# Copies of the sort's turned blocks moved from VectorE to ACT, in fixed chunks of the convolution's tiles

## The chip, the cores and the metric

The kernel runs on one core of one Trainium2 chip. The metric is the device time of one execution in microseconds (us). A core has five engines that run their own instruction streams and meet by semaphores: PE (TensorE, matrix products), VectorE (DVE), ACT (ScalarE), POOL (GpSimd) and SP (SyncE, here an issuer of transfers). Each works through its own stream in order: an instruction that waits holds up what stands behind it on its engine.

## The reference

The whole network is a convolution layer of 32 paths, an attention layer with a 7 x 7 window, and a graph layer with experts:

```python
x = _L0_conv_ref(x, ...)                  # 32 paths: 1x1 to 4 channels, 3x3, 1x1 to 64, each with norm and relu; sum + x, relu
t = _to_tokens(x)
t = t + _L1_attn_ref(_ln_t(t), ...)
t = t + _L1_ffn_ref(_ln_t(t), ..., L1_ffn_edge_index)   # graph attention over 262144 edges, then two of four experts a token
```

The graph layer sums over the edges that end in a node (`segment_sum(..., dst)`). The kernel sorts the 262144 edges by their end for it, and does that sort while the convolution of the first six images runs.

## The kernel before

`conv_phase` is called twice. The first call takes six images of 56 x 56 pixels, seven tiles of eight rows each, 42 tiles, and carries the sort; the second takes the last two images later and has no sort. All loops over tiles are written out, so each engine has one long fixed order of instructions.

**A tile of the convolution.** PE expands a stack of 75 rows to the 32 paths' 64 channels in 16 chunks (`expand`, L570), two chunks into each of two PSUM tiles `psE`. VectorE folds each pair of chunks with relu into `acc` (L882 for the first pair of a tile, L885 for the other seven). So a pair (called duo in the code) can be expanded only when the fold two pairs before has freed its PSUM tile. Between the chunks PE does other things of the tiles around: the nine taps of the 3 x 3 convolution of the tile three ahead, one behind each of chunks 4 to 12 (L553); the sum of the tile before (`to_tokens`, L593) behind chunk 3; the turn of its normalised tokens to channels behind chunk 4 (L604); the projection of the tile two before (L610, L615) behind chunk 13.

Each tile's layer norm goes through three engines. VectorE adds the residual (L825) behind its second fold; ACT takes relu with a sum (L689). VectorE makes the negated mean (L830) behind its fourth fold, that of chunks 6 and 7; ACT's squares of the tile (L697) wait for it. Variance (L834) and inverse deviation (L838, L840) follow behind the sixth and eighth fold.

ACT's order in a tile is fixed too: relu of the reduced input (L659), the normalised tokens (L707), a part of the split of a later tile and its store, relu with sum (L689), the copy of turned tokens (L712), squares (L697), `stack_parts` (nine transfers that load the stack of the tile two ahead, issued from ACT's queue at L682), relu behind the taps (L665, L667), the projection's copies (L719, L722, L727), the deviation (L702).

**The sort.** `Sort.plan` is a bitonic sort over 128 partitions of 2048 keys, in two buffers `sort_key` and `sort_other`. A compare step is two VectorE instructions of 1024 columns, the minima (L276) and the maxima (L278); signs and negations are single ones. Where the network compares across partitions, the whole array is turned: PE transposes blocks of 128 x 128, four at a time, into one PSUM bank `psFV` (`turn`, L316), and VectorE copies the bank out into the other buffer with a strided target (`copy_back`, L284). One turn is four such rounds, and there are 14 turns, 56 rounds. There is one bank for this, which `to_tokens` and `project` use as well: a round waits until the copy of the round before is done.

The 417 entries of the list (361 VectorE instructions, 56 rounds) are spread over slots of the tiles. The first 26 run ahead of the tiles. Slot `at` of a tile stands ahead of VectorE's fold `at // 2`; eleven slots a tile are in use, all of 2 to 13 but 4, and `schedule` gives one to a VectorE instruction and two to a round (the copy stands in the second, PE's turn behind the chunk one before it). So rounds can fall on any of chunks 1 to 12, one to three chunks apart, also ahead of the sum behind chunk 3.

Of the kernel before, what the change touches and what calls it, by code (L numbers as in the profile page):

```python
# [20 lines left out]
TILES = H // ROWS  # L21
# [115 lines left out]
SORT_SLOTS = (2, 3, 5, 6, 7, 8, 9, 10, 11, 12, 13)  # L137
# [85 lines left out]
class Sort:  # L223
# [32 lines left out]
    def vector_steps(self, dve, bank):  # L256
# [23 lines left out]
        def copy_back(now, turns, r):  # L280

            dve.wait_ge(self.turn_ready, turns * self.ROUNDS + r + 1)
            size = LOW // self.ROUNDS
            dve.tensor_copy(self.buffers[1 - now][:].rearrange("h (p l) -> h l p", l=LOW)[:, r * size:(r + 1) * size, :],  # L284
                            bank[:].rearrange("h (l p) -> h l p", p=128)).then_inc(self.turn_done, 1)

        for kind, *args in self.plan:
            if kind == "turn":
                for r in range(self.ROUNDS):
                    out.append((lambda a=(now, turns, r): copy_back(*a), (now, steps, turns, r)))  # L290
                turns += 1
                now = 1 - now
                continue
            for half in range(2 if kind == "compare" else 1):
                out.append((lambda a=(kind, args, now, steps, turns, half): one(*a), None))
            steps += 1
            if kind == "compare":
                now = 1 - now
        return out

    def schedule(self, marks):

        slot, at = 0, {}
        for k, mark in enumerate(marks):
            slot += 1 if mark is None else 2
            at[slot] = k
        return at
# [12 lines left out]
def conv_phase(nc, io, images, t1_dram, q_dram, kpad_dram, vpad_dram, sorted_dram=None, gate=None, kept_ident=None):  # L320
# [3 lines left out]
    with ExitStack() as ctx:  # L324
# [62 lines left out]
        sort_slots, turn_at = {}, {}  # L387
        if sorted_dram is not None:
            sort = Sort(sort_key, sort_other, signs, stepped, turn_ready, turn_done)
            marks = [mark for _, mark in sort.vector_steps(None, None)][SORT_FIRST:]  # L390
            sort_slots = sort.schedule(marks)
        for slot, k in sort_slots.items():
            if marks[k] is not None:
                turn_at[slot // len(SORT_SLOTS), SORT_SLOTS[slot % len(SORT_SLOTS)] - 1] = marks[k]

# [41 lines left out]
        with (nc.Block() if gate is None else nullcontext(gate.block)) as block:  # L437
# [95 lines left out]
            def _(pe):  # L533
# [29 lines left out]
                def expand(n, t, taps, others):  # L563
                    g = n * TILES + t
                    pe.wait_ge(stacked[t], 16 * 9 * (n + 1))
                    for c in range(CHUNKS):
# [8 lines left out]
                        if (g, c) in turn_at:  # L575
                            wait(pe, u_done, issued["folds"])
                            wait(pe, v_done, issued["values"])
                            sort.turn(pe, psTurn, ident, *turn_at.pop((g, c)))
                            issued["rounds"] += 1
# [61 lines left out]
                assert not turn_at  # L641
# [6 lines left out]
            def _(act):  # L648
# [79 lines left out]

                def image(n, first, last):
                    for t in range(TILES):  # L730
# [11 lines left out]
                        if not (first and t == 0):  # L742
                            squares(*ahead(n, t, -1))
                        if not (last and t + 2 >= TILES):
                            stack_parts(*ahead(n, t, 2))
                        if not (last and t + 3 >= TILES):
# [27 lines left out]
            def _(dve):  # L774
# [71 lines left out]
                if sorted_dram is not None:  # L846
# [6 lines left out]
                    steps = [step for step, _ in sort.vector_steps(dve, psTurn)]  # L853
                sort_at = {slot: steps[SORT_FIRST + k] for slot, k in sort_slots.items()}

# [11 lines left out]
                def tile(n, t, pending):  # L867
                    g = n * TILES + t
                    for duo in range(DUOS):
                        for k, at in enumerate(SORT_SLOTS):  # L870
                            if at // 2 == duo and g * len(SORT_SLOTS) + k in sort_at:
                                sort_at.pop(g * len(SORT_SLOTS) + k)()
# [31 lines left out]
                for at in sorted(sort_at):  # L904
                    sort_at[at]()
# [1463 lines left out]
```

## Time and profile before

| | us |
|---|---|
| median of 3 executions (5034.34 to 5045.57) | 5041.94 |
| the profiled execution's own time | 5049.61 |
| its span, first to last instruction | 5048.0 |
| VectorE busy in the span | 2727.8 (54%) |
| PE busy in the span | 2733.0 (54%) |
| ACT busy in the span | 1504.5 (30%) |

Busy time is the union of an engine's instructions; register work, waits and the issue of transfers don't count. The span is one execution on the one core. In rows of the trace a line begins with its start in us from the span's start, then its duration, engine, line of the kernel, operation and the tensors it writes and reads; what stands in brackets is the idle time ahead of it on its engine and who ended that. PEclk and "granted clock" are shares of TensorE's full clock of 2.4 GHz: 0.50 is 1.2 GHz.

### The profile page before, as it was taken

What the parts mean: (1) busy time and instruction counts of PE and PEld (TensorE: products, weight loads), DVE (VectorE), ACT (ScalarE), POOL (GpSimd) and SP (SyncE); (2) the same over time, 40 slices, a digit from 0 to 9 for tenths busy, and PEclk for the clock granted to TensorE, in tenths of its full rate; (3) what the DMA queues carried; (4) which work ended last, traced back from release to release, by engine and by line L of the source; (5) the groups of instructions that cost most, each with busy time, mean ns of one, the idle gap of its engine ahead of it and who ended that gap; (6) DMA issues with size and microseconds to landing.
All of it is one profiled execution on the core that took longest, in us unless ns stands there. A gap on an engine that the chain in (4) does not pass through costs nothing. (4 is left out here: it accounts for less than half of the span.)

```text
span 5048.0 us, 57429 instructions
## 1 busy us (share of the span) xinstructions
PE 2733.0 (54%) x15808; PEld 1889.2 (37%) x15808; DVE 2727.8 (54%) x4352; ACT 1504.5 (30%) x5774; POOL 2782.1 (55%) x3036
## 2 busy tenths in 40 slices
PE   5888888769999777858828853101210211021222
PEld 2454454458888655634418741000000000000122
DVE  7988889849999749954556661101110111001277
ACT  1333333348888410003416622101110111011100
POOL 1000000026667537776777777777777777777473
PEclk8877888769999755558757856555555555555565
DMA  5666666546666450126734432101110111011244
GB/s 98 99 106 99 99 104 107 83 77 103 101 104 102 85 148 11 11 52 99 117 82 82 83 80 78 45 8 45 45 45 8 46 45 43 9 42 41 83 149 145
DMA packets 620524, 380.12 MB, mean 75 GB/s; under 512 B 431448, under 2 KB 552344, under 8 KB 617656
## 3 DMA queue, kind: packets, MB, share of 16 engines
q1 hardware_dynamic: 425208, 223.43, 19.5%
q10 hardware_dynamic: 94368, 109.47, 12.4%
q0 software_dynamic: 100768, 45.27, 7.4%
q8 instruction: 58, 0.95, 0.1%
q14 instruction: 122, 1.00, 0.1%
HBM read 232.92 MB, written 144.35 MB: 75 GB/s over the span
## 5 line engine op out<-in xcount | busy, mean ns | idle before, releaser
L1603 POOL DMA_INDIRECT e_row<-scratch_table,e_edge x2048 | 2011.3, 982 | 680.9 <-issue 678.4
L1968 PE MATMUL f_psY<-f_hid,f_w 128*64 128x512 f32 x392 | 126.8, 745 | 1460.4 <-ACT f_hid L1928 1460.4
L1777 DVE TENSOR_TENSOR e_e<-e_row,e_b 128x512 f32<-128x512 f32 x16 | 11.3, 704 | 1528.1 <-DMA e_row<-scratch_table,e_edge 1527.8
L1968 PEld LDWEIGHTS f_psY<-f_hid,f_w 128*64 128x64 f32 x392 | 35.8, 157 | 1538.6 <-ACT f_hid L1928 1527.0
L1031 POOL MEMSET a_wproj<- 128x128 f32 x1 | 0.2, 209 | 1025.8 <-POOLq L179 1025.8
L1184 ACT ACTIVATE prob<-psS,low 128x100 f32<-128x100 f32 x1568 | 512.5, 371 | 104.2 <-DVE low L1219 102.6
L553 PE MATMUL psH<-h,c_w 128*128 128x448 f32 x1008 | 513.9, 602 | 8.1 <-ACT h L659 4.5
L1119 PE MATMUL psS<-keys,q_exp 84*128 84x100 f32 x3136 | 419.8, 288 | 156.9 <-DMA keys<-in_kfeat 154.0
L885 DVE SCALAR_TENSOR_TENSOR acc<-psE,acc 128x896 f32<-128x896 f32 x392 | 425.3, 1085 | 112.4 <-PE psE L570 105.2
L1119 PEld LDWEIGHTS psS<-keys,q_exp 84*128 84x128 f32 x3136 | 404.5, 208 | 161.1 <-issue 154.1
L1809 ACT ACTIVATE e_weight<-e_drop 128x1024 f32<-128x1024 f32 x16 | 16.9, 1056 | 1470.9 <-DVE e_drop L1790 1470.9
L570 PE MATMUL psE<-stack,c_w 75*128 75x448 bf16 x896 | 345.0, 429 | 158.6 <-DVE acc L885 128.8
L1184 ACT ACTIVATION_READ_ACCUMULATOR prob<-psS,low 128x1 f32 x1568 | 367.7, 234 | 0.0
L1701 DVE TENSOR_TENSOR i_hot<-i_values,i_digit 128x1024 bf16<-128x1024 bf16 x512 | 319.3, 700 | 0.3 <-DVE i_values L1693 0.3
L1219 DVE TENSOR_REDUCE low<-psS 128x5 f32<-128x500 f32 x336 | 212.5, 641 | 155.1 <-PE psS L1119 147.8
L1730 PE MATMUL i_psC<-i_hot 128*128 128x128 bf16 x2048 | 255.8, 298 | 71.7 <-DVE i_hot L1701 71.7
L553 PEld LDWEIGHTS psH<-h,c_w 128*128 128x128 f32 x1008 | 219.2, 218 | 122.0 <-issue 111.0
L1195 ACT ACTIVATE prob_t<-psP 100x512 f32<-100x512 f32 x448 | 227.6, 578 | 106.4 <-PE psP L1133 106.3
L1133 PE MATMUL psP<-a_ident,prob 128*100 128x128 f32 x1568 | 234.9, 292 | 37.2 <-ACT prob_t L1195 32.0
L1730 PEld LDWEIGHTS i_psC<-i_hot 128*128 128x128 bf16 x2048 | 190.1, 133 | 137.4 <-DVE i_hot L1701 137.4
L1028 POOL DMA_DIRECT2D scratch_t<-t x168 | 113.2, 678 | 193.3 <-DVE t L1261 99.1
L570 PEld LDWEIGHTS psE<-stack,c_w 75*128 75x128 bf16 x896 | 87.3, 112 | 348.5 <-issue 157.6
(297 smaller groups left out, 5507.7 us busy)
## 6 DMA issues: line engine op xcount, KB each, us to landing
stack<-scratch_parts ACTq DMA_DIRECT2D x504, 112.0 KB
e_row<-scratch_table,e_edge POOLq DMA_INDIRECT x2048
val<-scratch_vpad SPq DMA_DIRECT2D x784, 35.0 KB
scratch_y<-f_y ACTq DMA_DIRECT2D x49, 512.0 KB, 2.7
scratch_state<-e_state SPq DMA_DIRECT2D x16, 1536.0 KB, 6.3
g_y<-scratch_y SPq DMA_DIRECT2D x24, 1024.0 KB
scratch_parts<-h2p ACTq DMA_DIRECT2D x56, 336.0 KB, 6.4
keys<-scratch_kpad SPq DMA_DIRECT2D x112, 155.0 KB
```

What stands on the lines that cost most here:

```text
L553: m = pe.matmul(psH2[:, 0:PIX].rearrange("p (y x) -> p y x", x=W), w2[:, tap, :], h1[:, ROWS * t + dy:ROWS * (t + 1) + dy, dx:dx + W], sta ...
L570: m = pe.matmul(psE[duo % 2][:, half, 0:PIX], w3[:, c, :], stack[third(n, t)][:, c, :], start=True, stop=True)
L885: dve.scalar_tensor_tensor(acc[:, third(n, t)], e, 0.0, acc[:, third(n, t)], ALU.max, ALU.add).then_inc(stt_done, 1)
L1119: m = pe.matmul(psS[bank][:, (blk - a) * KEYS:(blk - a + 1) * KEYS], q_exp[st.pair][:, par, blk].rearrange("k h m -> k (h m)"), keys[st.at ...
L1133: m = pe.transpose(psP[k % 2][0:KEYS, (blk - a) * 128:(blk - a + 1) * 128], prob[par][:, blk * KEYS:(blk + 1) * KEYS], ident[:])
L1184: m = act.activation(prob[par][:, blk * KEYS:(blk + 1) * KEYS], psS[bank][:, (blk - a) * KEYS:(blk - a + 1) * KEYS], ACT.Exp, bias=low[par ...
L1195: act.activation(prob_t[:, a:b, :], psP[k % 2][0:KEYS, 0:(b - a) * 128].rearrange("k (b m) -> k b m", m=128), ACT.Copy).then_inc(pt_done, 1)
L1219: dve.tensor_reduce(low[par][:, a:b], psS[bank][:, 0:(b - a) * KEYS].rearrange("p (b k) -> p b k", k=KEYS), AX.X, ALU.min)\
L1603: pool.indirect_dma_start(out=self.row[s][:, f, :], out_offset=None, in_=self.table_dram, in_offset=bass.IndirectOffsetOnAxis(ap=self.edge ...
L1701: m = dve.tensor_tensor(hot[g % 2][d][:], values[:].unsqueeze(1).to_broadcast([128, HOT // 2, 128, 2]), digit[par][:, d, g * HOT:(g + 1) * ...
L1730: m = pe.matmul(psC, hot[g % 2][1][:, c // 2, :, c % 2], hot[g % 2][0][:, c // 2, :, c % 2], start=False, stop=False)
L1968: m = pe.matmul(psY[par][half:half + C, e // 2, :], w2[:, e, :], hid[e][:], start=True, stop=True)
```

## The change

The copies of the turned blocks go from VectorE to ACT (`copy_back` is now called in ACT's stream, by `copies_back`). Rounds may stand only behind chunks 6 to 11 of a tile (`ROUND_AT`), one chunk apart; VectorE steps may use all of the slots 2 to 13, also slot 4. `schedule` now walks both lists: a turn's first round comes at least two slots behind the step ahead of it, and a step at least three behind the last round. In ACT's order the copies of rounds behind chunks 6 and 7 stand between the squares and `stack_parts`, those behind chunks 8 to 11 between `stack_parts` and the relu behind the taps. By the new plan the sort's last step stands in tile 41, the last; before it stood in tile 40.

```diff
-SORT_SLOTS = (2, 3, 5, 6, 7, 8, 9, 10, 11, 12, 13)
+SORT_SLOTS = tuple(range(2, 14))
+ROUND_AT = tuple(range(6, 12))
...
-        def copy_back(now, turns, r):
-
-            dve.wait_ge(self.turn_ready, turns * self.ROUNDS + r + 1)
-            size = LOW // self.ROUNDS
-            dve.tensor_copy(self.buffers[1 - now][:].rearrange("h (p l) -> h l p", l=LOW)[:, r * size:(r + 1) * size, :],
-                            bank[:].rearrange("h (l p) -> h l p", p=128)).then_inc(self.turn_done, 1)
-
...
     def schedule(self, marks):
 
-        slot, at = 0, {}
+        tile, free, steps, rounds = 0, 0, {}, {}
         for k, mark in enumerate(marks):
-            slot += 1 if mark is None else 2
-            at[slot] = k
-        return at
+            if mark is not None and mark[3] == 0:
+                free += 2
+            allowed = SORT_SLOTS if mark is None else ROUND_AT
+            while not any(at >= free for at in allowed):
+                tile, free = tile + 1, 0
+            at = next(at for at in allowed if at >= free)
+            if mark is None:
+                steps[tile, at] = k
+            else:
+                rounds[tile, at] = mark
+            free = at + (3 if mark is not None and mark[3] == self.ROUNDS - 1 else 1)
+        return steps, rounds
+
+    def copy_back(self, act, bank, now, steps, turns, r):
+
+        act.wait_ge(self.turn_ready, turns * self.ROUNDS + r + 1)
+        size = LOW // self.ROUNDS
+        act.activation(self.buffers[1 - now][:].rearrange("h (p l) -> h l p", l=LOW)[:, r * size:(r + 1) * size, :],
+                       bank[:].rearrange("h (l p) -> h l p", p=128), ACT.Copy).then_inc(self.turn_done, 1)
...
-                        if (g, c) in turn_at:
+                        if (g, c) in rounds:
                             wait(pe, u_done, issued["folds"])
                             wait(pe, v_done, issued["values"])
-                            sort.turn(pe, psTurn, ident, *turn_at.pop((g, c)))
+                            sort.turn(pe, psTurn, ident, *rounds[g, c])
...
+                def copies_back(n, t, *at):
+                    for c in at:
+                        if (n * TILES + t, c) in rounds:
+                            sort.copy_back(act, psTurn, *rounds[n * TILES + t, c])
...
                             squares(*ahead(n, t, -1))
+                        copies_back(n, t, *ROUND_AT[0:2])
                         if not (last and t + 2 >= TILES):
                             stack_parts(*ahead(n, t, 2))
+                        copies_back(n, t, *ROUND_AT[2:])
                         if not (last and t + 3 >= TILES):
                             h2_relu(*ahead(n, t, 3))
```

On ACT, in tile 10, where the first turn stands by the new plan, the order before is this (`t` and `sq` are relu and squares of the tile before, `stack` the nine loads for the tile two ahead, `h` and `h2p` the relu behind the taps):

```order
L689 ACTIVATE t_0,stat<-usum 112x64 x4
L712 ACTIVATE z_ch<-psQK 64x448
L697 ACTIVATE sq,stat<-t_0,stat 112x64 x4
L682 DMA stack_0<-scratch_parts 8x16x448 x9
L665 ACTIVATE h_0<-psH_0,c_s_0 128x448
L667 ACTIVATE h2p<-h_0 128x448
```

And with the change (lines are numbered anew; L316 is the copy):

```order
L694 ACTIVATE t_0,stat<-usum 112x64 x4
L717 ACTIVATE z_ch<-psQK 64x448
L702 ACTIVATE sq,stat<-t_0,stat 112x64 x4
L316 ACTIVATE sort_other<-psFV 128x4x128 x2
L687 DMA stack_0<-scratch_parts 8x16x448 x9
L316 ACTIVATE sort_other<-psFV 128x4x128 x2
L670 ACTIVATE h_0<-psH_0,c_s_0 128x448
L672 ACTIVATE h2p<-h_0 128x448
```

Two copies now stand behind the squares, and two behind the nine loads. On PE, the turn that begins in tile 14 stood before as follows, from chunk 10 of tile 14 to the sum behind chunk 3 of tile 15 (`psE` are the chunks, `psH` the taps, `psFV<-c_ident` the turns):

```order
L570 MATMUL psE_0<-stack_0,c_w_0 128x448
L553 MATMUL psH_0<-h_0,c_w_0 128x448
L316 MATMUL psFV<-c_ident,sort_key 128x128 x4
L570 MATMUL psE_0<-stack_0,c_w_0 128x448
L553 MATMUL psH_0<-h_0,c_w_0 128x448
L570 MATMUL psE_0<-stack_0,c_w_0 128x448
L553 MATMUL psH_0<-h_0,c_w_0 128x448
L316 MATMUL psFV<-c_ident,sort_key 128x128 x4
...
L570 MATMUL psE_0<-stack_0,c_w_0 128x448 x3
L316 MATMUL psFV<-c_ident,sort_key 128x128 x4
L570 MATMUL psE_0<-stack_0,c_w_0 128x448
L593 MATMUL psFV<-c_fold,acc 112x64 x8
```

With the change it stands in chunks 6 to 9 of tile 14:

```order
L576 MATMUL psE_0<-stack_0,c_w_0 128x448
L559 MATMUL psH_0<-h_0,c_w_0 128x448
L326 MATMUL psFV<-c_ident,sort_key 128x128 x4
L576 MATMUL psE_0<-stack_0,c_w_0 128x448
L559 MATMUL psH_0<-h_0,c_w_0 128x448
L326 MATMUL psFV<-c_ident,sort_key 128x128 x4
L576 MATMUL psE_0<-stack_0,c_w_0 128x448
L559 MATMUL psH_0<-h_0,c_w_0 128x448
L326 MATMUL psFV<-c_ident,sort_key 128x128 x4
L576 MATMUL psE_0<-stack_0,c_w_0 128x448
L559 MATMUL psH_0<-h_0,c_w_0 128x448
L326 MATMUL psFV<-c_ident,sort_key 128x128 x4
```

The four rounds of a turn stood over two tiles, one of them ahead of the sum behind chunk 3; now they stand in neighbouring chunks of one tile, with a chunk and a tap between two of them.

## Rows read from the trace of the kernel before

**Rows 1.** Windows of stages: first:end, length, busy time (and instructions) of each engine, PEclk, transfers

```profile
core 0: us, PE busy (x) PEld busy (x) DVE busy (x) ACT busy (x) POOL busy (x), PEclk, DMA share, GB/s
...
74.62:1025.50 950.88, 795.53 (x2886) 459.70 (x2884) 855.00 (x1010) 341.87 (x1213) 0.00 (x0) 0.79 0.62 98
```

**Rows 2.** VectorE's groups in the stage: count, busy us, mean ns, idle ahead and releaser

```profile
L882 DVE TENSOR_SCALAR acc<-psE 128x896 f32<-128x896 f32 x42 | 45.5, 1083 | 9.8 <-PE psE L570 9.8
L284 DVE COPY sort_other<-psFV 128x512 f32<-128x512 f32 x28 | 28.4, 1014 | 15.5 <-PE psFV L316 15.2
L284 DVE COPY sort_key<-psFV 128x512 f32<-128x512 f32 x28 | 28.4, 1014 | 8.0 <-PE psFV L316 7.1
```

**Rows 3.** Windows of tile 13 and tile 33, columns as in group 1

```profile
371.20:393.83 22.63, 18.43 (x67) 10.18 (x66) 22.46 (x28) 8.54 (x32) 0.00 (x0) 0.80 0.69 105
...
834.65:854.28 19.63, 19.63 (x87) 12.85 (x85) 17.82 (x23) 8.40 (x32) 0.00 (x0) 0.85 0.62 97
```

**Rows 4.** Timeline of tile 33 (834.65 to 854.28) and of its successor's first product

```profile
834.69 3.11 PE L593 MATMUL psFV<-c_fold,acc 128*112 128x64 f32 x16
...
835.65 1.21 DVE L276 TENSOR_TENSOR sort_other<-sort_key 128x1024 f32<-128x1024 f32 x1
836.79 1.22 DVE L278 TENSOR_TENSOR sort_other<-sort_key 128x1024 f32<-128x1024 f32 x1
...
841.79 0.35 PE L570 MATMUL psE<-stack,c_w 75*128 75x448 bf16 x1
...
842.74 0.35 PE L570 MATMUL psE<-stack,c_w 75*128 75x448 bf16 x1
...
843.68 0.61 PE L316 MATMUL psFV<-c_ident,sort_other 128*128 128x128 f32 x4
...
844.13 0.35 PE L570 MATMUL psE<-stack,c_w 75*128 75x448 bf16 x1
...
844.14 0.16 DVE L830 TENSOR_SCALAR stat<-stat 112x4 f32<-112x4 f32 x1
...
844.33 0.35 ACT L697 ACTIVATE sq<-t,stat 112x64 f32<-112x64 f32 x1 [2.87 <-DVE stat L830]
...
845.00 0.27 ACTq L682 DMA_DIRECT2D stack<-scratch_parts  x1
...
845.58 0.19 ACT L697 ACTIVATION_READ_ACCUMULATOR sq<-t,stat 112x1 f32 x1
...
845.68 2.67 ACTq L682 DMA_DIRECT2D stack<-scratch_parts  x7
...
848.80 0.35 PE L570 MATMUL psE<-stack,c_w 75*128 75x448 bf16 x1
...
851.27 2.28 DVE L885 SCALAR_TENSOR_TENSOR acc<-psE,acc 128x896 f32<-128x896 f32 x2
...
851.73 0.55 PE L570 MATMUL psE<-stack,c_w 75*128 75x448 bf16 x2
...
853.99 1.70 PE L593 MATMUL psFV<-c_fold,acc 128*112 128x64 f32 x16
```

**Rows 5.** Timeline of a turn that waited for a VectorE step

```profile
501.40 1.28 DVE L271 TENSOR_SCALAR sort_other<-sort_other,signs 128x2048 f32<-128x2048 f32 x1
...
502.94 0.69 PE L316 MATMUL psFV<-c_ident,sort_other 128*128 128x128 f32 x4 [2.00 <-DVE sort_other L271]
...
503.67 1.01 DVE L284 COPY sort_key<-psFV 128x512 f32<-128x512 f32 x1
```

**Rows 6.** ACT's groups by form: a copy of 512 columns out of PSUM

```profile
L1547 ACT ACTIVATE t_z_ch<-t_psZ 64x512 f32<-64x512 f32 x28 | 16.4, 586 | 4.3 <-PE t_psZ L1519 4.3
```

**Rows 7.** Waits in the stage: who waited for whom, total us, times, longest us

```profile
ACT sq L697 <- DVE stat L830: 161.6, 41, 4.9
```

**Rows 8.** Windows of tile 33 before and after its change of clock, columns as in group 1

```profile
834.65:840.59 5.94, 5.94 (x26) 4.78 (x25) 5.22 (x7) 2.10 (x10) 0.00 (x0) 0.50 0.98 150
840.59:854.28 13.69, 13.69 (x63) 8.07 (x61) 12.59 (x16) 6.30 (x23) 0.00 (x0) 1.00 0.46 75
```

More of the change, by code:

```diff
@@ L254, in __init__, with vector_steps @@
         self.steps = sum(step[0] != "turn" for step in self.plan)
-    def vector_steps(self, dve, bank):
+    def vector_steps(self, dve):
         now, steps, turns = 0, 0, 0
@@ L289, in vector_steps @@
                 for r in range(self.ROUNDS):
-                    out.append((lambda a=(now, turns, r): copy_back(*a), (now, steps, turns, r)))
+                    out.append((None, (now, steps, turns, r)))
                 turns += 1
@@ L386, in conv_phase @@
         turn_ready = sem("turn_ready"); turn_done = sem("turn_done")
-        sort_slots, turn_at = {}, {}
+        sort_slots, rounds = {}, {}
         if sorted_dram is not None:
             sort = Sort(sort_key, sort_other, signs, stepped, turn_ready, turn_done)
[L390 to L394, printed above, removed]
+            sort_slots, rounds = sort.schedule([mark for _, mark in sort.vector_steps(None)][SORT_FIRST:])
         psH1 = ps("psH1", [128, 512])
@@ L640, in _ @@
                     image(n, n == 0, n == N - 1)
-                assert not turn_at
                 to_tokens(N - 1, TILES - 1)
@@ L852, in _ @@
                     dve.wait_ge(built, 2)
-                    steps = [step for step, _ in sort.vector_steps(dve, psTurn)]
+                    steps = [step for step, _ in sort.vector_steps(dve)]
                 sort_at = {slot: steps[SORT_FIRST + k] for slot, k in sort_slots.items()}
+                assert all(g < N * TILES for g, at in sort_at)
                 def rest(n, t):
@@ L869, in tile @@
                     for duo in range(DUOS):
-                        for k, at in enumerate(SORT_SLOTS):
-                            if at // 2 == duo and g * len(SORT_SLOTS) + k in sort_at:
-                                sort_at.pop(g * len(SORT_SLOTS) + k)()
+                        for at in SORT_SLOTS:
+                            if at // 2 == duo and (g, at) in sort_at:
+                                sort_at.pop((g, at))()
                         if g + 2 < N * TILES:
@@ L903, in _ @@
                     op()
-                for at in sorted(sort_at):
-                    sort_at[at]()
+                assert not sort_at
         if gate is None:
```

## Prediction

> **What bounds the kernel now.** I read the windows by stage first. The stretch from the first to the last fold of the early convolution takes 950.88 us, and VectorE is busy in 855.00 of them (90%), more than any other engine [rows 1]; what comes behind the stage in the span of 5048.0 us holds none of the changed code. So only this stage can move, and VectorE is its bound, with 95.9 us of idle time in it. Then I read VectorE's groups: the 56 copies that the change takes away are 2 x 28.4 us of busy time, and VectorE stood 15.5 + 8.0 us in front of them [rows 2]. Last I read single tiles. A tile with eleven sort steps and no round is VectorE's alone: 22.46 busy of 22.63 us. A tile with four rounds is not: in tile 33 (834.65 to 854.28) PE is busy for all of its 19.63 us and VectorE for 17.82 [rows 3]. So the copies cost VectorE's time in some tiles, and in tiles with rounds the order of PE and of what PE waits for decides. That is where the change has to be priced.
>
> **What the new plan makes of the tiles.** By the new schedule the same 335 VectorE steps and 56 rounds fall into three kinds of tile. 25 tiles have no round (17 of them twelve steps). Nine (10, 11, 14, 18, 22, 32, 34, 37, 39) have two steps, at slots 12 and 13, and four rounds, at chunks 6 to 9. Eight have something between: 15 and 19 four rounds and four steps, 23 and 24 two rounds, 27 and 29 three, 26 and 28 one. What VectorE saves: a copy lasts 1.014 us [rows 2], and neighbours overlap by some 0.08 us (a step lasts 1.21 us, the next starts 1.14 later [rows 4]), so 56 x 0.934 = 52.3 us of busy time go. The other term is the idle time in tiles with rounds, worked out by walking through one.
>
> **A tile of two steps and four rounds.** I use tile 33, whose PE work is the same (four rounds, at chunks 5, 7, 9 and 11, and three steps, at slots 2, 3 and 13), and count from its start at 834.65. PE reaches the second turn at 843.68, that is at 9.03 [rows 4], with one turn and the products of chunks 4 to 7 before it, exactly what stands before it in the new order. In the new order this turn needs the first copy, and on ACT that copy stands behind the squares of the tile before. The squares wait for VectorE's negated mean, which comes behind the fold of chunks 6 and 7: it starts at 844.14, the squares at 844.33, and the last of them ends at 845.77, at 11.12 [rows 4]. This is no accident of one tile: ACT waited for that value 41 times, 3.9 us each on average [rows 7]. So the first copy starts at 11.12, some 3 us after its block is turned (PE does that before chunk 7, which starts at 842.74, at 8.09).
>
> What a copy costs on ACT no row shows. Low end: ACT copies 512 contiguous columns out of PSUM in 0.586 us [rows 6]. High end: VectorE's copy with the very same strided target, 1.014 us [rows 2]. VectorE passes 896 contiguous columns of PSUM in 1.083 us [rows 2], so 512 would be 0.62, and the stride costs it 0.39 us; I add these to ACT's 0.586 and take 0.98 us, nearer to the row with the same target. The Trainium skill prices it too (ScalarE: Activation LUTs, What ACT_TABLE_LOAD costs): 186 ns and 0.833 ns a column with immediate scale and bias, an estimate of 0.61 us here, with no word of the target's stride. The contiguous row agrees with it; by it alone the sum below would be about 10 us lower.
>
> The copy ends at 12.10. From VectorE's last write to a waiting turn the trace shows 0.26 us (502.68 to 502.94), a turn of 0.69, and 0.04 to the copy [rows 5]. The second turn thus starts at 12.36 instead of 9.03: **3.33 us late**. It ends at 13.05, ACT takes its copy at 13.09, and only then may ACT's queue issue the nine loads of the next stack that stand behind it. These nine take from 845.00 to 848.35, 3.35 us [rows 4], so the third copy, behind them, starts at 16.44 and ends at 17.42, and the fourth turn starts at 17.68. PE alone would have come to it two chunks after the second turn, at 2 x 1.39 us (842.74 to 844.13 is a chunk with tap and turn [rows 4]), at 15.14: **2.54 us late** once more. Together 5.87 us.
>
> Tile 33 starts chunk 12 at 848.80, at 14.15, with four turns behind it; here that is 20.02, and chunk 11 one pair (0.95 us, 841.79 to 842.74) earlier, with its product done at about 19.42 [rows 4]. VectorE folds chunks 10 and 11 to 20.55, makes its two steps (2 x 1.14) to 22.85, and folds the last two pairs; from the first of these to the next tile's start tile 33 needs 3.01 us (851.27 to 854.28). The tile is 25.86 us long. PE doesn't prolong it: its chunks 14 and 15 end 3.48 us after chunk 12 starts (848.80 to 852.28), at 23.5, and VectorE wants them at 23.95. VectorE's own work in it is 22.46 - 9 x 1.14 = 12.2 us, so **13.7 us idle, nine times: 123 us**. The eight mixed tiles walked the same way, each wait where its own slots put it: 15 is 25.4 us long (bound by PE's end), 19, 24, 27 and 29 about 25, 23 is 23.2, 26 and 28 19.6; against their work 10.9, 10.5, 10.5, 11.6, 11.6, 6.5, 1.5 and 1.5 us idle, 65 us.
>
> **Sum.** 855.0 - 52.3 + 123 + 65 + 25 x 0.2 (tile 13's rest of 0.17 [rows 3]) = 995.7 us for a stage that took 950.9: **45 us longer**. The waits in front of the old copies and the folds that stood behind them are gone in this sum; they are among the 95.9 us that I replaced. The added wait on the loads of the stack costs nothing by itself: they are issued some 2 to 3 us later for a tile two tiles ahead. Twelve steps instead of eleven in a tile cost nothing beyond their own 1.14 us. The profiled execution took 5049.6 us; the median of three is 5041.9, and I put the 45 us on that: **5087 us**.
>
> Bounds. With a copy of 0.59 us the first and the third wait are 0.39 shorter in 14 tiles: -11 us. The start of tile 33 ran at 1.2 GHz for 5.94 us, with PE busy throughout [rows 8]; the same fold took 3.11 us there and 1.70 at 2.4 GHz [rows 4]. If every such tile began at 2.4 GHz its second turn could come 3.0 us earlier at most: -42 us in 14 tiles. Both together leave about -8. The other way, a fall of the clock is the second rival.
>
> **Rivals.**
> *The copies are in time* (the other side). If PE hardly waited, a tile with four rounds would be tile 33 and one step more, 20.8 us: 8.6 us idle nine times (77), about 37 in the mixed tiles: 855.0 - 52.3 + 77 + 37 + 5 = 922, 29 us shorter, 5013 us. For it speaks that ACT is busy for only 8.4 us of such a tile [rows 3]. Against it, that ACT's order is fixed: the first copy can't pass the squares, nor the third the nine loads. It decides where the two waits come to 2.3 us a tile instead of 5.87. Chance 0.12.
> *The clock falls in the wait.* In tile 33 PE ran without a pause and the clock held 2.4 GHz from 840.59 to the end [rows 8]. Here PE stands for over 3 us in the middle. If the clock then went to 1.2 GHz, the 8.15 us of products from 844.13 to 852.28 [rows 4] would double, and some 3 us of that fit into the second wait and VectorE's lead: 5 us a tile, 70 us in 14, about 35 if half of them fall: 5122 us. The Trainium skill (TensorE: Matmul & The Clock Gate, Part 1) says that the throttled state is the default and activity releases it; the rows at the tile's start bear that out, none that I read shows such a pause in mid-tile. Chance 0.15.
> *The waits are there but shorter* (cheap copy, tiles that begin at 2.4 GHz, a chunk 7 that comes earlier): 3 to 25 us slower, 5045 to 5067 us. Chance 0.25, of which a third is within 0.2%.
>
> **How the numbers follow.** 0.2% (10 us) is about what a measurement of this kernel can tell from no change. My forecast, 25 to 68 us slower, has 0.48, with 5067 to 5110 as its own range. With the rivals: slower 0.78, same 0.10, faster 0.12. The range runs from 5040, which leaves out the faster rival, to 5130, which leaves out the worse half of the clock rival.
>
> **What would show it.** Right, if VectorE's busy time in the stage falls to about 803 us while the stage gets longer; if the tiles named above last about 26 us and the others about 24; if PE waits about 3 us for ACT's copy before the second turn and 2 to 3 before the fourth; and if ACT's third copy starts right behind the ninth load. Wrong, if ACT's squares end before PE has turned the first block (the negated mean comes earlier than at 9.5), if the third copy starts while the loads are still being issued, or if the tiles with rounds are under 22 us. A copy of 0.6 or 1.0 us settles the price of the stride.

## The result, and the profile after

The changed kernel takes 5094.0 us (median of four executions, 5086.52 to 5100.35) against 5043.75 us (four, 5034.34 to 5046.36): ratio 1.0096, interval 1.0083 to 1.0109. It is some 50 us slower; 5087 was predicted.

The windows of the changed kernel, columns as in [rows 1]: the stage (this window is 0.6 us wider than from the first to the last fold), a tile of twelve sort steps and no round, and a stretch of the last part of the network, long behind the stage.

```profile
73.77:1062.30 988.53, 775.37 (x2890) 433.67 (x2887) 800.61 (x955) 397.08 (x1270) 0.00 (x0) 0.82 0.60 94
...
358.90:382.55 23.65, 18.91 (x67) 10.61 (x66) 23.51 (x28) 8.54 (x32) 0.00 (x0) 0.79 0.63 103
4789.53:4826.10 36.57, 36.57 (x72) 11.90 (x72) 8.12 (x18) 17.47 (x27) 0.00 (x0) 0.64 0.29 111
```

From the first to the last fold it is 987.9 us, 37.0 us longer than the stage in [rows 1]. VectorE lost some 54 us of work (855.00 to 800.61) as the diff promises; its idle time grew from 95.9 to 187.6 us. The view of VectorE's waits says for whom it stood (who waited for whom, total us, times, longest us):

```profile
DVE acc L898 <- PE psE L576: 171.6, 60, 8.2
DVE acc L895 <- PE psE L576: 8.0, 1, 8.0
DVE h2p L878 <- ACT h2p L676: 7.0, 13, 0.9
```

Nearly all of it is the fold waiting for PE's chunks, up to 8.2 us at a time. The same view for all engines says why PE was late, and why ACT was:

```profile
ACT sq L702 <- DVE stat L842: 172.1, 41, 5.6
...
PE psFV L326 <- ACT sort_key L316: 36.9, 18, 5.2
PE psFV L326 <- ACT sort_other L316: 32.3, 13, 3.1
...
ACT sort_other L316 <- issue: 18.4, 6, 4.9
ACT sort_key L316 <- issue: 17.2, 5, 5.8
```

PE's turns stood 69.2 us for ACT's copies; ACT's squares stood 172.1 us for VectorE's negated mean (161.6 before [rows 7]); and 35.6 us ahead of a copy ACT waited for "issue", which is its own queue at the nine loads. So the ring is closed: VectorE waits for PE, PE for ACT, ACT for VectorE.

Tile 10 (309.25 to 336.02) shows it from row to row:

```profile
317.96 0.61 PE L326 MATMUL psFV<-c_ident,sort_key 128*128 128x128 f32 x4
...
319.80 0.16 DVE L842 TENSOR_SCALAR stat<-stat 112x4 f32<-112x4 f32 x1
320.00 0.35 ACT L702 ACTIVATE sq<-t,stat 112x64 f32<-112x64 f32 x1 [4.41 <-DVE stat L842]
...
321.34 1.00 ACT L316 ACTIVATE sort_other<-psFV 128x512 f32<-128x512 f32 x1
...
322.48 0.69 PE L326 MATMUL psFV<-c_ident,sort_key 128*128 128x128 f32 x4 [2.97 <-ACT sort_other L316]
...
323.21 1.03 ACT L316 ACTIVATE sort_other<-psFV 128x512 f32<-128x512 f32 x1 [0.87 <-PE psFV L326]
323.21 3.36 ACTq L687 DMA_DIRECT2D stack<-scratch_parts  x9
...
325.30 1.09 DVE L898 SCALAR_TENSOR_TENSOR acc<-psE,acc 128x896 f32<-128x896 f32 x1 [5.33 <-PE psE L576]
326.62 1.02 ACT L316 ACTIVATE sort_other<-psFV 128x512 f32<-128x512 f32 x1 [2.39 <-issue]
...
327.79 0.69 PE L326 MATMUL psFV<-c_ident,sort_key 128*128 128x128 f32 x4 [1.78 <-ACT sort_other L316]
```

The first block is turned by 318.57 and lies in the bank for 2.8 us until ACT, held in the squares, takes it out at 321.34; PE stands 2.97 us. The third copy starts at 326.62, right behind the ninth load. Something that the prediction did not have appears in tile 18 (497.8 to 525.3), where the loads themselves are late:

```profile
500.10 0.35 ACTq L680 DMA_DIRECT2D scratch_parts<-h2p  x1
...
507.57 1.02 ACT L316 ACTIVATE sort_key<-psFV 128x512 f32<-128x512 f32 x1 [0.87 <-PE psFV L326]
...
510.93 3.40 ACTq L687 DMA_DIRECT2D stack<-scratch_parts  x9
514.37 1.02 ACT L316 ACTIVATE sort_key<-psFV 128x512 f32<-128x512 f32 x1 [5.77 <-issue]
...
515.54 0.66 PE L326 MATMUL psFV<-c_ident,sort_other 128*128 128x128 f32 x2 [5.17 <-ACT sort_key L316]
```

The nine loads read what the store at 500.10 writes, and in the code ACT waits for its landing ahead of them. The view of the DMA issues gives that store 10.8 us to landing in this window:

```profile
scratch_parts<-h2p ACTq DMA_DIRECT2D x1, 336.0 KB, 10.8
```

That is 510.90, and the loads start at 510.93. ACT's queue stood from 508.59 until then with nothing to do, and the third copy behind it. So it is in four of the nine tiles with two steps and four rounds: in tiles 14, 18, 32 and 37 the loads start 0.02 us after the landing, in the other five together with the second copy.

### The profile page after: what moved, and what is told of

It is laid out like the page before. It is cut to its first block and busy times, and to the rows that moved or that the text cites. A ratio compares the mean times of both kernels' runs of the same rounds, so it can differ in the third digit from the quotient of the medians.

```text
span 5098.6 us, 57429 instructions
## 1 busy us (share of the span) xinstructions
PE 2718.7 (53%) x15808; PEld 1864.4 (37%) x15808; DVE 2674.2 (52%) x4296; ACT 1562.3 (31%) x5830; POOL 2783.9 (55%) x3036
```

## The experiments

The times of each set stand beside runs of the kernel before on the same chip (medians 5043.75 for the changed kernel, 5049.99, 5051.12 and 5050.19 us for the three sets of experiments, each of which ran on another chip), so the ratios are what is compared from set to set: 0.001 is 5 us. Stage is first to last fold, of one profiled execution each; the run on the copy's price below has the changed kernel's stage unchanged and took 984.4 us for it against 987.9, so differences of a few us of stage are not told from chance. The nine tiles are those with two steps and four rounds in the new plan.

| kernel | us | ratio, interval | stage | VectorE busy | mean of the nine |
|---|---|---|---|---|---|
| before | | 1 | 950.9 | 855.0 | 22.1 |
| changed | 5094.0 | 1.0096 (1.0083 to 1.0109) | 987.9 | 800.4 | 25.9 |
| two copies ahead of the squares | 5086.25 | 1.0069 (1.0057 to 1.0081) | 975.8 | 800.4 | 25.3 |
| two copies ahead of the loads | 5068.94 | 1.0034 (1.0018 to 1.0051) | 964.0 | 800.2 | 22.6 |
| both | 5036.09 | 0.9973 (0.9963 to 0.9983) | 935.0 | 801.2 | 20.5 |
| new plan, copies on VectorE | 5022.56 | 0.9942 (0.9928 to 0.9956) | 924.2 | 850.3 | 20.4 |
| all four ahead of the squares | 5047.27 | 0.9994 (0.9983 to 1.0004) | 941.0 | 802.4 | 20.6 |
| two chunks apart | 5067.97 | 1.0039 (1.0025 to 1.0054) | 955.8 | 801.3 | (another plan) |
| two apart, all ahead of the loads | 5081.26 | 1.0064 (1.0051 to 1.0077) | 981.4 | 800.7 | (another plan) |
| changed, neighbours together | 5082.35 | 1.0066 (1.0053 to 1.0079) | 976.5 | 799.7 | 25.3 |
| both, neighbours together | 5032.34 | 0.9963 (0.9950 to 0.9975) | 935.2 | 801.2 | 20.3 |
| copies on VectorE, neighbours together | 5020.37 | 0.9945 (0.9934 to 0.9957) | 918.0 | 833.9 | 19.9 |

**The theory** is that of the prediction: ACT's fixed order makes PE wait twice in a tile of rounds. Rivals: the new plan's crowding of four rounds into one tile costs the time whoever copies; the copy's price on ACT does; the clock does.

### The first wait alone: two copies ahead of the squares

```diff
+                        copies_back(n, t, *ROUND_AT[0:2])
                         if not (first and t == 0):
                             squares(*ahead(n, t, -1))
-                        copies_back(n, t, *ROUND_AT[0:2])
```

> Changed kernel, but in ACT's order the copies of the rounds behind chunks 6 and 7 stand ahead of the squares; those of chunks 8 to 11 stay behind the nine loads. Theory A (the two places in ACT's order cost the time): the second turn starts about 9.4 us into a tile with four rounds instead of 12.4, but the squares and with them the nine loads end only 1.2 us earlier, and the fourth turn waits for them: 1.2 us less in nine tiles and some in the mixed ones, 12 to 20 us less than the changed kernel, about 33 us above the kernel before (5077). The stage (first to last fold) about 972 us. Theory B (the pace: rounds one chunk apart, each behind a copy of 1.02 us, whatever stands around them): within 8 us of the changed kernel, about 47 above before. Theory C (PE's clock falls while it waits): the time follows the granted clock in the tiles with rounds.

The stage is 12.1 us shorter than the changed kernel's, the ratio 0.0027 (14 us) lower. The first copies now come at once, but the time saved is partly given back at the second wait. Tile 14 of this kernel starts at 401.1:

```profile
408.16 1.02 ACT L316 ACTIVATE sort_other<-psFV 128x512 f32<-128x512 f32 x1 [0.87 <-PE psFV L326]
...
409.33 0.68 PE L326 MATMUL psFV<-c_ident,sort_key 128*128 128x128 f32 x4 [0.26 <-ACT sort_other L316]
...
413.91 3.34 ACTq L687 DMA_DIRECT2D stack<-scratch_parts  x9
417.30 1.02 ACT L316 ACTIVATE sort_other<-psFV 128x512 f32<-128x512 f32 x1 [6.91 <-issue]
418.46 1.09 PE L326 MATMUL psFV<-c_ident,sort_key 128*128 128x128 f32 x4 [7.51 <-ACT sort_other L316]
```

PE is done with its third turn at 410.01, 8.9 us into the tile, and behind one more chunk and tap it stands 7.51 us ahead of the fourth: the store of this tile, issued at 403.4, landed 10.5 us later, and nothing behind the loads could start before. The loads start at the landing in eight of the nine tiles now, and most of the first wait has moved to the second: in the nine tiles PE's waits ahead of the second turn fall from 27.5 to 3.1 us in all, and those ahead of the fourth grow from 21.4 to 44.1. All of PE's waits for copies in this stage, 69.2 us before the edit, come to 59.7:

```profile
PE psFV L326 <- ACT sort_key L316: 34.2, 19, 7.0
...
PE psFV L326 <- ACT sort_other L316: 25.5, 18, 7.5
```

### The second wait alone: two copies ahead of the loads

```diff
                         copies_back(n, t, *ROUND_AT[0:2])
+                        copies_back(n, t, *ROUND_AT[2:])
                         if not (last and t + 2 >= TILES):
                             stack_parts(*ahead(n, t, 2))
-                        copies_back(n, t, *ROUND_AT[2:])
```

> Changed kernel, but all copies of a tile stand between the squares and the nine loads. Theory A: the first wait stays (second turn at 12.4 or later), the third copy follows its turn at once and the fourth turn starts at about 16.3 instead of 17.7: 12 to 18 us less than the changed kernel, about 35 us above the kernel before. The nine loads are issued 3 us later, with no effect. Theory B: within 8 us of the changed kernel. A rival on the loads: if their issue were the tight part, the tile two later would wait for its stack and the time would rise above the changed kernel.

23.9 us off the stage, 0.0062 (31 us) off the ratio, more than the 12 to 18 us that were expected. PE's waits for copies fall by about as much as the stage, to 44.9 us:

```profile
PE psFV L326 <- ACT sort_key L316: 22.5, 13, 3.7
PE psFV L326 <- ACT sort_other L316: 22.4, 13, 3.0
```

What is left is the first wait, which is the larger of the two in all; removed alone, it gave only 12.1 us of stage because the second took most of it back.

### Both

The first two copies ahead of the squares, the other two between squares and loads.

> Changed kernel, with the copies of chunks 6 and 7 ahead of the squares and those of chunks 8 to 11 between the squares and the nine loads. Theory A: both waits shrink, the fourth turn starts at about 13.9 instead of 17.7; 42 to 50 us less than the changed kernel, which is more than the sum of the two single edits (24 to 38), because in each of them the other wait takes over; within 15 us of the kernel before. Theory B: 10 to 15 us less than the changed kernel at most. Theory C: the gain goes with a higher granted clock in the tiles with rounds.

52.9 us off the stage, 0.0123 (62 us) off the ratio. That is more than the two edits apart (12.1 + 23.9), as the first one's gain needs the second: what an edit is worth hangs on the order, 12.1 and then 40.8 us of stage, or 23.9 and then 29.0. The new plan with the copies on ACT is faster than the kernel before now (0.9973). PE's waits for copies, which were 69.2 us:

```profile
PE psFV L326 <- ACT sort_key L316: 9.8, 21, 1.2
PE psFV L326 <- ACT sort_other L316: 5.8, 18, 0.5
```

They fell by 53.6 us, the stage by 52.9. Since chunk for chunk the rounds stand as in the changed kernel, the plan's crowding is not what cost the time there. The stage's granted clock is 0.83 against 0.82, but single tiles differ: in the changed kernel the clock falls to 1.2 GHz in the middle of seven of the nine (11, 14, 18, 22, 32, 34 and 37); here those seven hold 2.4 GHz from 7 us on until 17.7 us or later. So the falls of the clock come and go with the waits and are a part of their price; the part on why the prediction was right says how large.

### The plan alone: copies back on VectorE

```diff
-        act.activation(self.buffers[1 - now][:].rearrange("h (p l) -> h l p", l=LOW)[:, r * size:(r + 1) * size, :],
-                       bank[:].rearrange("h (l p) -> h l p", p=128), ACT.Copy).then_inc(self.turn_done, 1)
+        dve.tensor_copy(self.buffers[1 - now][:].rearrange("h (p l) -> h l p", l=LOW)[:, r * size:(r + 1) * size, :],
+                        bank[:].rearrange("h (l p) -> h l p", p=128)).then_inc(self.turn_done, 1)
...
+                            if at // 2 == duo and (g, at - 1) in rounds:
+                                sort.copy_back(dve, psTurn, *rounds[g, at - 1])
```

ACT's two calls of `copies_back` are left out.

> The changed kernel's plan (rounds behind chunks 6 to 11, steps in all slots from 2 to 13), but the copies made by VectorE again, each in the slot behind its round; ACT as in the kernel before. Theory A: no copy stands behind squares or loads, so a tile with four rounds lasts about 21.4 us; VectorE has its 52 us of copies back; all in all 0 to 15 us below the kernel before, so some 55 us less than the changed kernel. Theory B: the copy costs 1.01 us on VectorE as 1.02 on ACT and the rounds are as close together, so about the time of the changed kernel, 40 to 50 us above before.

More than that: 27 us under the kernel before, and by the medians under every version with the copies on ACT (the interval of the nearest, 0.9963 in the table, overlaps with this one's by 0.0006). The window of its stage (0.6 us wider than first to last fold), and VectorE's wait for the chunks in it:

```profile
73.96:998.79 924.83, 758.00 (x2889) 422.88 (x2887) 850.54 (x1011) 339.23 (x1214) 0.00 (x0) 0.84 0.65 100
```

```profile
DVE acc L898 <- PE psE L576: 16.3, 15, 2.7
```

VectorE does 49 us more work here than with both earlier places on ACT, and the stage is 10.8 us shorter. So the change falls into two parts: the new plan gives 26.7 us of stage (950.9 to 924.2), and handing the copies to ACT where the diff puts them takes 63.7 (924.2 to 987.9). In the nine tiles of four rounds, 20.4 us long on average, PE is busy for 18.5 us and VectorE, copies and all, for 16.2, so its copies can cost little there. Why the plan itself gains was not taken apart: it packs the rounds, uses slot 4 and has no round ahead of the sum behind chunk 3 any more, where PE waited 15.9 us for copies in the kernel before (8.8 and 7.1 us, by its view of waits) and waits for none here.

### All four ahead of the squares

> The changed kernel with all copies of a tile ahead of the squares, and so ahead of the nine loads. Theory A: nothing is left in front of a copy but its own turn, so it is the lower end for copies on ACT in this plan; against the kernel with both edits only the third copy could gain (its turn waited 0.1 to 0.2 us for the squares there), while the squares now end some 3 us later and VectorE's variance behind the sixth fold may wait up to 1 us: within 8 us of that kernel, 5 to 20 us below the kernel before. If it came out clearly faster than the kernel with both edits, the squares still held copies up there; if slower, the variance waits.

It is 6.0 us of stage and 0.0021 (11 us) of the ratio worse than with two of them behind. PE's wait for copies hardly differs (12.7 against 15.6 us); but now the squares wait for the last round, and VectorE's variance for the squares:

```profile
DVE stat L846 <- ACT sq L702: 9.1, 5, 2.9
```

With two behind the squares that wait was at most 1.5 us, so it could cover the 6 us; but PE's wait for input tiles that SP's queue loads (`x_tok`) is 4 us longer here too (13.6 against 9.6), and no run tells the two apart.

### The price of the copy

At the end of the stage of the changed kernel, 24 more copies from the bank, four of each form: 512 elements side by side; every second; every fourth, eighth, sixteenth (rows of 128, as in the kernel's own copy); and every sixteenth group of four neighbours, written neighbour after neighbour:

```diff
+    act.activation(flat[:, 0:128 * stride].rearrange("h (p l) -> h l p", l=stride)[:, 0:4, :],
+                   psTurn[:].rearrange("h (l p) -> h l p", p=128), ACT.Copy)
+    act.activation(flat[:, 0:2048].rearrange("h (p l) -> h p l", l=16)[:, :, 0:4],
+                   psTurn[:].rearrange("h (l p) -> h p l", p=128), ACT.Copy)
```

> The changed kernel with 24 more copies at the very end of ACT's stream in the stage, out of the sort's PSUM bank into a buffer no longer needed, each waiting for the one before; four of each kind, 512 columns: contiguous target; stride of 2; four runs of 128 with a stride of 4, 8 and 16 (the last is the sort's own pattern); and the sort's own target written four neighbours at a time, the source strided instead. They change nothing that is computed. If the stride is what makes ACT's copy 1.02 us, the contiguous one takes 0.59 to 0.65 us and the price rises with the stride up to 1.02 at 16; if it is the bank, the partitions or ACT itself, all kinds take about 1.02. In the last kind neighbours are written together: 0.6 to 0.7 us if the order of writes counts, 1.0 if the span does. The time is that of the changed kernel and some 20 us.

Groups of ACT by line (duration ns min/median/max): side by side; every second; the three larger strides together; neighbours together.

```profile
L788 ACT ACTIVATE h<-psFV x4: 591/597/597, 1075.6 to 1077.5; 128x512 f32<-128x512 f32 x4
```

```profile
L790 ACT ACTIVATE h<-psFV x4: 619/619/619, 1078.1 to 1080.1; 128x512 f32<-128x512 f32 x4
```

```profile
L793 ACT ACTIVATE h<-psFV x12: 1023/1066/1084, 1080.7 to 1092.8; 128x512 f32<-128x512 f32 x12
```

```profile
L796 ACT ACTIVATE h<-psFV x4: 597/597/597, 1093.8 to 1095.7; 128x512 f32<-128x512 f32 x4
```

Its single run took 5097.25 us. The price is not one of distance: between strides of 8 and 16 bytes it jumps from 0.62 to 1.07 us, and stays within 1.02 to 1.08 at 16, 32 and 64 bytes. Writing four neighbours one after the other brings it back to 0.60, though PSUM is then read 128 columns apart; nor are the shorter runs the reason, as this form has the shortest. The Trainium skill (SBUF — State Buffer, Door 1: The DMA port swizzle, the remark on lines) says that accesses which follow one another run at full rate when at least two fall in the same line of 16 bytes. The rows agree on both sides of that step.

The same order of writing in the kernels:

```diff
-        act.activation(self.buffers[1 - now][:].rearrange("h (p l) -> h l p", l=LOW)[:, r * size:(r + 1) * size, :],
-                       bank[:].rearrange("h (l p) -> h l p", p=128), ACT.Copy).then_inc(self.turn_done, 1)
+        act.activation(self.buffers[1 - now][:].rearrange("h (p l) -> h p l", l=LOW)[:, :, r * size:(r + 1) * size],
+                       bank[:].rearrange("h (l p) -> h p l", p=128), ACT.Copy).then_inc(self.turn_done, 1)
```

In the changed kernel:

> The changed kernel with one edit: ACT's copy walks its target so that the four elements that lie side by side are written one after the other (and reads PSUM 128 columns apart), instead of 512 writes 64 bytes apart. A look at such copies alone gave 0.60 us in place of 1.02. If the copy's price is a term of the two waits in a tile with four rounds, the second and the fourth turn each come some 0.4 us earlier in 9 tiles and parts of that in the mixed ones: stage 7 to 12 us shorter than that of the changed kernel, time 5082 to 5088 us, and PE's waits for ACT's copy fall from 69 to about 57 us. Rival: only the order on ACT decides (squares, loads and the landing of the store ahead of them), and the loads take up what the copy gives back: stage within 4 us.

```profile
L316 ACT ACTIVATE sort_other<-psFV x28: 572/597/597, 321.3 to 836.4; 128x512 f32<-128x512 f32 x28
```

The stage is 11.4 us shorter, as the prediction's bound for a cheap copy had it (11 us), the ratio 0.003 lower. PE's waits fell less than expected, from 69.2 to 63.6 us and not to 57: ACT's own wait at the loads ahead of its copies grew from 35.6 to 58.3 us. So half of the 11.4 us does not show in PE's waits, and where it comes from is open. With both earlier places:

> The copies on ACT at both earlier places in its order (two ahead of the squares, two ahead of the loads), with the four neighbours written together. There PE's waits for copies are only some 16 us in all, so the copy's price can give back little: 0 to 8 us below the same kernel with the old order of writing (ratio 0.996 to 0.9975). If it gives 10 us or more, the copy's 0.4 us counts elsewhere on ACT: in the squares, the relu of the next tile and the loads behind it.

The stage is the same (935.2 against 935.0) and the times' intervals overlap: the copy's price gives nothing that this measurement can tell. PE's waits for copies did fall, from 15.6 to 3.5 us, but its waits for `x_tok` were 7.5 us longer in this profile (17.1 against 9.6), so a gain of some us may be hidden. And on VectorE:

> The new plan with the copies on VectorE, and their target walked four neighbours at a time. If VectorE's copy too is slowed by its writes 64 bytes apart, it falls from 1.01 to about 0.62 us, VectorE's busy time in the stage from 850 to about 828, and the time by 3 to 15 us below the kernel with the copies on VectorE in the old order (in tiles with four rounds PE is the bound, so most of it turns into idle time of VectorE). Rival: on VectorE the reading of PSUM 128 columns apart costs as much as the writing did, the copy stays near 1.0 and the time within 4 us.

```profile
L316 DVE COPY sort_other<-psFV x28: 681/688/693, 315.4 to 789.2; 128x512 f32<-128x512 f32 x28
```

VectorE's copy falls from 1.01 to 0.69 us, its busy time by 16 us and the stage by 6.2; the ratio (0.9945) can't be told from that without it (0.9942), and 6.2 us of stage is not far above what chance gives.

### The rounds two chunks apart

An attempt to give each copy more time, on the kernel with both earlier places: one of the later two copies ahead of the loads, one behind.

```diff
-SORT_SLOTS = tuple(range(2, 14))
-ROUND_AT = tuple(range(6, 12))
+SORT_SLOTS = tuple(range(2, 16))
+ROUND_AT = (5, 7, 9, 11)
```

> Copies on ACT, but rounds only behind chunks 5, 7, 9 and 11, two chunks apart, and VectorE steps in the slots 2 to 15 so that the sort still ends in time (tile 40); copies of chunks 5 and 7 ahead of the squares, of 9 between squares and loads, of 11 behind the loads. With a turn, a copy and the way back 1.9 to 2.0 us after another, no turn should wait for a copy. Theory A (places in ACT's order): little more to gain than from both edits, since the turns there wait only 0.5 us each; the stage 920 to 935 us, 10 to 25 us below the kernel before. Theory B in its weak form (the pace of neighbouring chunks costs a good part): well below that, under 910 us and 40 us below the kernel before.

A miss: 20.8 us of stage more than with neighbouring chunks, all of it idle time of VectorE (154.5 against 133.8 us). The first thing to suspect was the last copy behind the loads, so it was put ahead of them too:

> The rounds two chunks apart (chunks 5, 7, 9, 11) as in the run that missed, with one edit: the last copy stands ahead of the nine loads too. If that run missed because its fourth copy stood behind the loads, which wait for the landing of the store and hold the sort's last steps and PE's next use of the bank, the tiles with four rounds fall from 23.2 us on average to 20 to 21, and the time to 5035 to 5052 us. Rival: the distance of two chunks itself costs (steps pushed to the end of the tile and into other tiles, the clock): then it stays within 6 us of 5068.

That is worse by 25.6 us of stage and 0.0025 of the ratio (13 us), so the suspicion falls. Two tiles are over 30 us long there, and the view of waits names the cause of some 16 of the 25.6 us, PE's wait for the input tiles `x_tok` (24.3 us, against 8.7 in the run ahead of it):

```profile
PE psH L549 <- DMA x_tok<-in_x: 24.3, 2, 13.0
```

Why these loads landed late, and why two chunks between rounds cost 20 us in the first place, stays open. What can be seen is that most turns now spread over two tiles, that tiles without rounds get fourteen steps (25.7 us), and that the stage's granted clock is lower than with neighbouring chunks (0.79 against 0.83); no run tells these apart.

## Why the prediction was right

**VectorE's work.** 802.7 us was worked out (855.0 - 52.3), 800.4 measured.

**The copy.** 0.98 us was taken for ACT, nearer to the row with the same target than to the contiguous one; it took 1.02 (28 each at 1023 and 1022 ns). The price list above shows the reason for that choice to be sound: the order of writing sets it, on both engines (0.43 us a copy on ACT, 0.33 on VectorE, by the runs with neighbours together). The price by contiguous columns would have been out by 0.4 us a copy.

**The first wait.** Its cause is shown by the rows of tile 10 and by the edit that removes it. The second turn was put at 12.36 us into the tile; in tile 10 it starts at 13.23 (322.48). Tile 18 ran at 2.4 GHz from its start, and its second turn starts at 9.05 (506.85), 3.3 us earlier than in the sum; the prediction's bound for this was 3.0. Tiles 11, 14, 32 and 37 began like it. The wait itself was put at 3.33 us; PE stood 3.05 on average in the nine tiles (2.97 in eight of them, 3.72 in tile 39).

**The second wait came out on average, but with a cause that the prediction lacks.** The step reads: "the third copy, behind them, starts at 16.44". With 3.35 us of issue and nothing that holds the loads up, that is near in tile 10 (17.37, behind a second turn that was 0.87 late). But the loads also wait for the landing of the store that ACT's queue issued ahead of the squares, 6.5 us in the middle of 40 and up to 12.9. Before the change only the relu behind the taps stood behind this wait. In tiles 14, 18, 32 and 37, which began fast, the second copy was done 1.1 to 2.3 us before the landing, and PE stood 2.9 to 5.2 us ahead of the fourth turn, where 2.54 was priced; in the other five it stood 0.4 to 1.9. The mean of the nine is 2.37 us, close to the price, but by chance. I called the loads' wait free because I asked only when their tile needs them, and not for how long a queue in order stands in front of them. The run with two copies ahead of the squares shows what that omission is worth: 12 us of stage where the first wait alone came to 27.5 in the nine tiles.

**Why the sum holds all the same.** The nine tiles came out at 25.85 us on average, predicted 25.86, though by errors against each other. Five tiles began at 2.4 GHz and reached the second turn 3.3 us early. In one of them, tile 11, the store landed in time, and the tile is 22.9 us long. The other four lost it again: 2.3 to 3.4 us between the second and the fourth turn, which is the late landing, and 1.4 to 1.8 us behind the fourth, where the clock had fallen during the wait (from the fourth turn's start to the tile's end they need 9.6 to 10.0 us, against 8.2 in tiles 10, 11, 22 and 34 and in the prediction). So the nearness is chance. The eight mixed tiles came to 183.7 us (about 188 predicted; tile 24, put at about 25, took 21.3), the others to 571.6 (575 in the sum), so the stage is 987.9 and not 995.7 us, 37 longer and not 45.

**Outside the stage.** That nothing else could move was the second flaw, and it hid the first shortfall: the rest of the span is 13.6 us longer in the profiled execution (5098.6 - 987.9 = 4110.7 against 5048.0 - 950.9 = 4097.1). Most of it is one stretch of 72 products near the end, 36.57 us above against the following in the kernel before, with the same instructions:

```profile
4747.38:4773.40 26.02, 26.02 (x72) 9.29 (x72) 8.12 (x18) 16.97 (x27) 0.00 (x0) 0.91 0.42 156
```

The granted clock was 0.91 there and 0.64 here: the stretch starts at 1.2 GHz, behind 141 us without work for PE, and goes to 2.4 GHz after 4.9 us there and only after 26.6 us here, with PE busy all the while in both by the profile. It does not go with the code: in the profiles of eight experiments, with the same code behind the stage, PE is busy with these two lines for 26.2 to 27.3 us from 4650 us on (27.1 in the kernel before), in two for 32.4 and 32.6, and here for 37.7. The four executions of the changed kernel lie in two pairs, 5086.5 and 5087.8, and 5100.3 and 5100.4; the profiled one is of the upper pair. Whether this stretch makes the pairs is not shown.

**The rivals.** The copies were not in time; they would have been, and the kernel faster, in the order that the run with both earlier places has. The clock did fall in the tiles of rounds: in tile 18, behind PE's long wait, the windows give

```profile
515.30:518.70 3.40, 3.16 (x9) 2.03 (x10) 0.00 (x0) 1.13 (x2) 0.00 (x0) 0.50 0.58 63
518.90:525.30 6.40, 6.17 (x28) 2.93 (x27) 6.25 (x10) 4.15 (x10) 0.00 (x0) 1.00 0.63 72
```

1.2 GHz in the first of these windows and 2.4 again in the second. In mid-tile it was so in seven of the nine tiles and five of the mixed, 51 us in all. So the second rival's mechanism is there, though not at its price: PE was busy for 47 of these 51 us, so the loss is by estimate at most half of that, 24 us, and what can be read off directly is 6 us, behind the fourth turn of tiles 14, 18, 32 and 37. Over the whole stage the clock was still higher than before (0.82 against 0.79).

## What to carry to other kernels

Work that is moved to an idle engine takes that engine's place in line with it: before moving it, list what the new queue waits for ahead of it, transfers included, and walk one tile with these waits. An engine at 90% of a stage is not its bound in every tile; here the copies on VectorE cost little in the tiles in which they stood (with copies a third cheaper such a tile took 19.9 us in place of 20.4), and the plan that packs them there was worth 27 us, more than any version that took them away. And a wait that is removed alone can come back at the next one in the same queue: the two edits here gave 36 us of stage apart and 53 together. Where a copy scatters, write neighbours one after the other.

## What the runs showed of the hardware

Not expected were the step in the price of a strided write between 8 and 16 bytes (0.62 to 1.07 us for 512 columns on ACT), its absence when four neighbours are written together (0.60 on ACT, 0.69 in place of 1.01 on VectorE), and that reading PSUM 128 columns apart cost nothing beside it on ACT. Nor was a stretch of unchanged code near the end of the program that took 26.0 us in one profiled execution and 36.6 in another, as the clock stayed at 1.2 GHz for 4.9 us of PE's work in the one and for 26.6 us in the other.
